# The eight middle turns of a software pipeline, in a loop of two turns or written out

## What is computed

```python
x = x + layernorm(attn(layernorm(x)))      # RWKV-like block with spiking neurons
x = x + layernorm(ffn(layernorm(x)))       # gated MLP, 128 -> 512 -> 512 -> 512 -> 128

# attn(x)
x = x + lif(time_mix(layer_norm(x)))       # k, v, r products, wkv scan over time, Wo product
x = x + lif(channel_mix(layer_norm(x)))    # square(relu(x Wk)) Wv, gated by sigmoid(x Wr)
# lif: v = v + (x_t - v)/2; s = (v >= 1); v = v*(1-s)   (a scan over time, spikes out)
# ffn(x)
h = silu(x W1 s1) * (x W2 s2); h = gelu(h H1 s3); h = gelu(h H2 s4); out = h W3 s5
```

## Time and profile before

| what | value |
|---|---|
| median of three runs | 690.81 us (690.18 to 691.85) |
| profiled execution | 692.57 us |
| its span, first to last instruction | 690.4 us |
| busy: PE, DVE, ACT, POOL | 594.9, 591.0, 536.2, 445.8 us |
| mean granted clock of TensorE | 0.973 of full speed |
| turns 6 to 13 | from 175.25 to 478.27 us |

### The profile page before, as it was taken

How to read it: one execution, slowest core, us unless ns; L and a number is a source line. 1 busy time by engine, 2 the same in 40 slices (tenths; PEclk the granted TensorE clock), 3 DMA queues, 4 the chain that set the end, 5 groups by cost and what they waited for, 6 DMA issues and landing times. The chain is left out here.

```text
span 690.4 us, 10811 instructions
## 1 busy us (share of the span) xinstructions
PE 594.9 (86%) x2241; PEld 368.2 (53%) x2241; DVE 591.0 (86%) x1596; ACT 536.2 (78%) x849; POOL 445.8 (65%) x576
## 2 busy tenths in 40 slices
PE   1247479999999989999899989999999999989883
PEld 0023136565656647565566646575656565656662
DVE  2875969999999979999899979999999999975631
ACT  4845367988979887979689887979797988858672
POOL 4332454697778666877678766868778684745352
PEclk9998679999999999999999999999999999999997
DMA  6110010001010100101010100001010101000000
GB/s 217 61 31 2 0 31 16 17 17 31 17 31 17 32 2 16 30 16 31 16 30 16 30 16 23 9 15 31 16 31 1 32 2 31 16 1 16 1 16 15
DMA packets 26553, 16.93 MB, mean 25 GB/s; under 512 B 1152, under 2 KB 25728, under 8 KB 26240
## 3 DMA queue, kind: packets, MB, share of 16 engines
q1 hardware_dynamic: 26496, 16.34, 7.8%
HBM read 12.14 MB, written 4.19 MB: 24 GB/s over the span
## 5 line engine op out<-in xcount | busy, mean ns | idle before, releaser
L782 ACT ACTIVATE hid<-p_f,scale 128x512 f32<-128x512 f32 x128 | 88.0, 687 | 70.1 <-PE p_f L1739 69.7
L1739 PE MATMUL p_f<-a_lo,w_hi 128*128 128x512 f32 x320 | 132.9, 415 | 2.9 <-DVE a_lo L295 1.7
L1739 PE MATMUL p_f<-a_hi,w_hi 128*128 128x512 f32 x320 | 125.8, 393 | 0.0
L1739 PE MATMUL p_f<-b_lo,w_hi 128*128 128x512 f32 x256 | 112.0, 438 | 4.0 <-DVE b_lo L295 3.0
L1739 PE MATMUL p_f<-b_hi,w_hi 128*128 128x512 f32 x256 | 100.5, 393 | 0.0
L776 ACT ACTIVATE a_hi<-hid 128x512 fp32r<-128x512 f32 x128 | 79.1, 628 | 12.0 <-DVE hid L1269 10.3
L429 POOL TENSOR_TENSOR rstd<-var,minus_half 128x4 f32<-128x4 f32 x64 | 84.3, 1318 | 2.5
L445 POOL TENSOR_TENSOR nd<-factors,pq 128x512 f32<-128x512 f32 x32 | 39.2, 1226 | 56.5 <-DVE pq L1129 56.4
L295 DVE TENSOR_TENSOR a_lo<-hid,a_hi 128x512 fp32r<-128x512 f32 x96 | 64.0, 691 | 11.2 <-ACT a_hi L776 11.0
L1739 PEld LDWEIGHTS p_f<-a_lo,w_hi 128*128 128x128 f32 x320 | 60.2, 188 | 22.6 <-issue 7.5
L1724 PE MATMUL p_m<-kk,mix 128*128 128x512 f32 x128 | 66.3, 625 | 3.8 <-issue 3.8
(11 more groups left out here) (141 smaller groups left out, 1501.3 us busy)
## 6 DMA issues: line engine op xcount, KB each, us to landing
xa<-in_x SPq DMA_DIRECT2D x16, 256.0 KB, 2.8
xb<-in_x SPq DMA_DIRECT2D x16, 256.0 KB, 3.1
out<-y_out SPq DMA_DIRECT2D x16, 256.0 KB, 3.0
kk<-in_ffn SPq DMA_DIRECT2D x1, 1024.0 KB, 6.3
hid<-in_ffn SPq DMA_DIRECT2D x1, 1024.0 KB, 8.8
mix<-in_mix SPq DMA_DIRECT2D x1, 512.0 KB, 6.5
gate<-in_ffn SPq DMA_DIRECT2D x1, 512.0 KB, 4.0
mix<-in_mix SPq DMA_DIRECT2D x1, 320.0 KB, 3.8
```

The lines of the kernel that those rows point to most:

```text
L782: act.activation(hid[:, m], p_f[m % 2][:, :], ACT.Gelu, scale=scale[:, 1 + layer, m:m + 1]).then_inc(s_gelu[layer], 1)
L1739: last = pe.matmul(out_, w[:, b], x[:, k], start=(k == 0 and t == 0), stop=(k == n - 1 and t == len(terms) - 1))
```

## The change

`Group` gets a flag `edge`. For all engines but PE's `program(True)`, `schedule` is called with None in place of the engine's loop, and the turns 6 to 13 are then written out one after the other with Python integers and `edge=False`. PE's additional waits go by `g.edge` in place of `isinstance(g.n, int)`, so that they stay out of the middle turns. `program(True)` keeps its loop. The order of work within a turn, the buffers and what each wait asks for are unchanged.

```diff
 class Group:
-    def __init__(self, pair, step):
+    def __init__(self, pair, step, edge=True):
         self.n = 2 * pair + step
+        self.edge = edge
...
-            def groups(pair, step):
-                return {k: Group(pair, step - k) for k in range(-2, 5)}
-            loop = range(6, GROUPS - 2)
+            def groups(pair, step, edge=True):
+                return {k: Group(pair, step - k, edge) for k in range(-2, 5)}
+            steady = range(6, GROUPS - 2)
             for i in range(first, last + 1):
-                if i == loop[0]:
-                    with fori(loop[0] // 2, len(loop) // 2 + loop[0] // 2) as pair:
-                        turn(groups(pair, 0), on(6))
-                        turn(groups(pair, 1), on(7))
-                elif i not in loop:
+                if i in steady and fori is None:
+                    turn(groups(i // 2, i % 2, False), on(i))
+                elif i == steady[0]:
+                    with fori(steady[0] // 2, len(steady) // 2 + steady[0] // 2) as pair:
+                        turn(groups(pair, 0, False), on(6))
+                        turn(groups(pair, 1, False), on(7))
+                elif i not in steady:
                     which = first_turn if i < 3 else turn if i < GROUPS else last_turn
                     which(groups(i // 2, i % 2), on(i))
...
-            schedule(sp.Fori, turn, turn, turn)
+            schedule(None, turn, turn, turn)
...
-            schedule(pool.Fori, first_turn, turn, last_turn)
+            schedule(None, first_turn, turn, last_turn)
...
-            schedule(act.Fori, first_turn, turn, last_turn)
+            schedule(None, first_turn, turn, last_turn)
...
-            schedule(dve.Fori, first_turn, turn, last_turn)
+            schedule(None, first_turn, turn, last_turn)
...
                 def turn_1(g):
                     pe.wait_ge(s_n[1], g.n + 1)
                     after(pe, s_f_out, g.n - 4)
-                    if isinstance(g.n, int):
+                    if g.edge:
                         after(pe, s_f0_lo, g.n - 3)
...
-                schedule(pe.Fori, first_turn, turn, last_turn, **turns)
+                schedule(pe.Fori if general else None, first_turn, turn, last_turn, **turns)
```

## The result

| kernel | median us (range, runs) | ratio to before | 95% interval |
|---|---|---|---|
| before | 691.33 (690.18 to 692.0, 4) | 1 | |
| after | 683.39 (682.53 to 685.62, 4) | 0.9892 | 0.9863 to 0.9921 |
| after, timed again on another occasion | 683.89 (683.77 to 685.13, 5) | 0.9906 | 0.9891 to 0.9921 |

The change makes the kernel faster by 1.1%, 7.9 us in the first comparison and 7.1 in the second (690.96 before); 682.8 us had been predicted. The profiled execution of after took 683.96 us, with a span of 681.8.

The account below looks back on a forecast made before the run. DVE was taken to bound the kernel, with fetch holes after three jumps back. Gaining 9.43 us there and losing 1.44 in odd turns gives 8.0 us less, from 690.81 to 682.8 us; range 679.2 to 686.

Parts of the forecast that it names:

- The bound: In the loop's turns, DVE has half a microsecond of slack per turn; its delays come out almost one for one.
- The holes as fetching: At the loop's jumps back, DVE stands still 3.56, 3.61 and 3.35 us, taken to be fetching its code anew.
- 9.43 us for the three jumps: Turns 8, 10 and 12 against turn 6's 36.88 us: 2.91, 3.80 and 2.72 us gained without DVE's jumps back.
- 1.44 us lost in the odd turns: Four odd loop turns go from 36.52 to 36.88 us, as POOL's `rstd` power takes 2.60 us, not 1.39.
- Nothing for register instructions, PE's waits and longer code: In the middle turns, dropped register arithmetic, PE's unchanged waits and fetching longer code were each taken as 0 us.
- The first rival: Middle turns: the odd ones keep 36.52 us, or all eight get it; 681.4 or 679.9 us; chance 0.18.
- Turn 10's clock: Turn 10's granted clock of 0.96, after PE waited for DVE, was to return to 1.00 without that wait.

Follow-up runs that it names:

- the hint: The kernel before, with hint_back_edge=True on DVE's loop, a hint for the code at the loop's head: 682.19 us.
- the count of jumps: From after, DVE alone loops, with a body of four turns run twice, so one jump back in place of three: 685.79 us, ratio 0.9937.
- two increments: After, with two semaphore increments on POOL's sequencer ahead of `d<-z`, putting it off by some 0.16 us: 677.17 us, ratio 0.9797; timed again 677.06 us.
- with one: After, with one semaphore increment on POOL's sequencer ahead of `d<-z`, a delay of some 0.08 us: 684.63 us, ratio 0.9902.
- with four: After, with four semaphore increments on POOL's sequencer ahead of `d<-z`, some 0.33 us of delay: 692.41 us, ratio 1.0025.

## Why the prediction was right

- **The bound.** DVE's slack of half a microsecond a turn, read from busy time against length, held: each hole of DVE came out in the turn, at 2.1 to 2.9 us for holes of 2.7 to 3.6 with the clock at 1.00, each against a turn of 36.9.
- **The holes as fetching.** Right as far as the runs reach: the hint, the count of jumps and ACT all agree with it, and no other account of the holes is left. No run shows a fetch itself. That ACT's short body escaped for its length was the right reading.
- **9.43 us for the three jumps.** The turns 8, 10 and 12 are 2.86, 3.75 and 2.66 us shorter than they were, 9.27 in all.
- **1.44 us lost in the odd turns.** 1.92 by the profile: 147.99 − 146.07 for turns 7, 9, 11 and 13. The step that named a reason failed: it was not DVE's waits that are issued earlier, since with DVE written out the odd turns stayed short. In these kernels it went with where POOL's `d<-z` begins, which the loops of POOL and of other engines put off; ACT's loop alone does so by 0.07 us, and that of PE was not tried alone. The prediction's starts that "agree within 0.01 us" are those of the power against DVE's products; `d<-z`, two instructions before it, began 1.83 and 1.75 us ahead in turns 6 and 7. Why that start decides the race was not found, and two turns with a start of 2.16 us and a short power do not fit a single bound. The 0.36 us a turn were put on `n<-xres` alone, and the `mixed` products are a part of the price.
- **Nothing for register instructions, PE's waits and longer code.** With only DVE written out the time is no longer than with all written out (681.49 and 683.39 us); between 150 and 520 us of after no wait of DVE, ACT, POOL or PE's matmuls ends by "issue", POOL's branches included, though PE's queue moves 23 packets in place of 16.
- **The first rival** (odd turns keep their speed, 681.4 us) is what two other kernels do: 681.49 with only DVE written out, 682.19 with the hint. By turns alone the prediction gave 295.04 us for the eight, and they took 295.73. That the first comparison of the times, 7.9 us, came within 0.1 of the predicted 8.0 is in part luck; the second gave 7.1.
- **Turn 10's clock.** Named as following PE's wait for DVE; the kernel with DVE alone in the loop fits, with 0.96, 0.96 and 0.92 in its three turns. Why the clock held in turns 8 and 12 of before, with holes as long, was not found.

## What to carry to other kernels

Cut the trace at an instruction that comes once a turn before reading shares: three turns were too long here, and one wait by "issue" named the engine. Where an engine that bounds runs a long loop body, write that engine's body out or hint the jump, and leave the others their loops. Then look for instructions whose length jumps between two values: 0.53 us of each turn hung on two engines meeting, and two increments at the right place were worth 6.8 us, almost as much as the whole change. What decides such a meeting is not understood here, so the delay has to be tried and not reckoned.

## What the runs showed of the hardware that was not expected

- A hole of DVE of 3.6 us costs more than itself when the granted clock falls in the turn in which PE waits behind it: in the kernel before 40.68 us for the turn at 0.96, against 39.60 and 39.79 at 1.00; in the kernel with DVE alone in the loop 42.18 us at 0.92.
- A power over 128x4 elements on POOL takes 1.00 us alone and 1.39 or 2.60 beside DVE; between the kernels with one and with two increments the start of an earlier instruction differs by under 0.1 us (1.79 to 1.81 us against 1.74 to 1.75).
- The same delay is worth −6.7 us with two increments, nothing with one and +8.5 with four (677.17, 684.63 and 692.41 against 683.9).
